# An adaLN Mamba and mixture-of-experts block: the small products of dt, router logits and sums of squares gathered into one row per pair of tiles

## Reference

```python
dt = jax.nn.softplus(dt + dt_bias)
y  = _ssd(x, dt, A, Bm, Cm) + x * D
y  = y * silu(z)
y  = y * rsqrt(mean(y * y, axis=-1) + EPS) * norm_w
x  = x + ga * (y @ W_out)
gate_logits = softmax(h2 @ gate_w + gate_b)
out = sum_e weights[:, e] * (h2 @ expert_w[e] + expert_b[e])
```

## Time and profile before

| what | value |
| --- | --- |
| runs | 2198.18, 2197.79, 2201.4 us, median 2198.18 |
| the profiled execution | span 2195.2 us from first to last instruction |
| what lies around the span, against the median | 3.0 us |
| PE busy | 2138.3 us (97%), 16090 matmuls |
| DVE, ACT, POOL busy | 1761.4 (80%), 1750.8 (80%), 1682.2 (77%) |
| mean granted TensorE clock | 0.992 of full |

### The profile page before, as it was taken

One profiled execution on the slowest core, in us unless ns is written; L12 is line 12 of the kernel. 1 busy time (PEld: TensorE's weight loads), 2 busy tenths in 40 slices (PEclk: granted clock), 3 DMA queues, 4 the chain that ended last, 5 costly groups with the idle time before them and its releaser, 6 DMA issues.

```text
span 2195.2 us, 51248 instructions
## 1 busy us (share of the span) xinstructions
PE 2138.3 (97%) x16090; PEld 1781.6 (81%) x16090; DVE 1761.4 (80%) x4001; ACT 1750.8 (80%) x4402; POOL 1682.2 (77%) x1812
## 2 busy tenths in 40 slices
PE   6799999999999999999999999999999999999997
PEld 5678888888888888888888888888888888888875
DVE  7778778887778888788888788888788887788863
ACT  5788887888887888888888888888888888888872
POOL 3568787777787777787777787777787777787786
PEclk9899999999999999999999999999999999999998
DMA  4221222222222222222222222222212222222210
GB/s 138 88 78 52 83 62 66 88 79 64 83 62 67 88 79 63 83 62 67 88 75 67 83 62 67 88 74 68 83 62 67 88 70 72 80 65 67 78 56 20
DMA packets 152204, 161.03 MB, mean 73 GB/s; under 512 B 15128, under 2 KB 134528, under 8 KB 151936
## 3 DMA queue, kind: packets, MB, share of 16 engines
q1 hardware_dynamic: 150160, 157.63, 23.4%
q10 hardware_dynamic: 1776, 0.12, 0.1%
HBM read 139.88 MB, written 17.83 MB: 72 GB/s over the span
## 4 chain that ended last, share of the span: by engine, by line
PE 89%; issue 3%; POOL 3%; DVE 3%; ACT 2%; DMA 0%; POOLq 0%; SPq 0%; DVEq 0%; ACTq 0%
PE pe L1320 32%; PE pa L1320 22%; PE pd L1320 12%; PE px L1320 10%; PE py L1320 6%; PE px L1432 3%; PE pa L1338 1%; PE pd L1491 1%; DVE feat L933 1%; PE py L1423 1%; POOL xd L423 0%; POOL ex L474 0%; POOL ex L479 0%; POOL ex L485 0%; POOL ex L470 0%
## 5 line engine op out<-in xcount | busy, mean ns | idle before, releaser
L933 DVE SCALAR_TENSOR_TENSOR feat<-pa,cw,feat 128x512 f32<-128x512 f32 x567 | 423.8, 747 | 83.5 <-ACT feat L609 73.1
L1320 PE MATMUL pe<-e_hi,h_hi 128*128 128x512 f32 x1024 | 443.7, 433 | 3.7 <-DVE eacc L1124 2.0
L1320 PE MATMUL pe<-e_lo,h_hi 128*128 128x512 f32 x1024 | 405.2, 396 | 0.0
L1320 PE MATMUL pe<-e_hi,h_lo 128*128 128x512 f32 x1024 | 404.4, 395 | 0.0
L1320 PE MATMUL pa<-h_hi,w_hi 128*128 128x260 f32 x1260 | 371.8, 295 | 6.3 <-DVE feat L933 5.7
L1320 PE MATMUL pa<-h_hi,w_lo 128*128 128x260 f32 x1260 | 357.8, 284 | 0.0
L1320 PE MATMUL pa<-h_lo,w_hi 128*128 128x260 f32 x1260 | 357.0, 283 | 0.0
L681 ACT ACTIVATE lm<-lm,lndt 128x128 f32<-128x128 f32 x1024 | 329.7, 405 | 2.5
L671 ACT ACTIVATE lm<-lm,e3in 128x128 f32<-128x128 f32 x1024 | 324.6, 405 | 1.1 <-DMA lm<-cs_rows 1.1
L761 ACT ACTIVATE ex<-pe,wg 128x256 f32<-128x256 f32 x512 | 215.0, 478 | 114.7 <-PE pe L1320 93.1
L1124 DVE SCALAR_TENSOR_TENSOR eacc<-pe,wg,eacc 128x256 f32<-128x256 f32 x512 | 244.3, 477 | 31.8 <-PE pe L1320 22.8
(11 more groups left out here) (184 smaller groups left out, 5659.3 us busy)
## 6 DMA issues: line engine op xcount, KB each, us to landing
lm<-cs_rows SPq DMA_DIRECT2D x128, 512.0 KB, 4.0
ebc<-cs_rows SPq DMA_DIRECT2D x256, 128.0 KB, 3.6
xin<-_attn_hidden_states_dram SPq DMA_DIRECT2D x32, 512.0 KB, 5.1
xres<-_attn_hidden_states_dram SPq DMA_DIRECT2D x128, 128.0 KB, 3.7
out_dram<-x SPq DMA_DIRECT2D x128, 128.0 KB, 3.9
gz<-in_L_wmod_dram SPq DMA_DIRECT2D x2, 512.0 KB, 8.2
ex<-in_L_ffn_expert_w_dram SPq DMA_DIRECT2D x1, 1024.0 KB, 11.5
x<-in_L_ffn_expert_w_dram SPq DMA_DIRECT2D x1, 1024.0 KB, 13.9
```

What stands on the lines that cost most here:

```text
L933: dve.scalar_tensor_tensor(out=acc, in0=proj_bank(x, i)[:, :, 1 + j:1 + j + HT], scalar=cw[:, f, j:j + 1], in1=acc, op0=ALU.mult, op1=ALU. ...
L1320: return pe.matmul(o, lhsT=l, rhs=r, start=start, stop=stop, skip_group_check=True)
```

## The change

Steps `dtm`, `dt2`, `lgm_`, `lg2`, `ssr_`, `ss_` on PE, `dte`, `lge`, `sre_` on ACT and `dtb`, `lg_`, `sse_` on DVE go. In their place stands one chain per pair: `mix`, `mixe`, `mix2`, `mixr`. `mix` of index c adds into the same four strips of `pd[:, 0]` the dt products of pair c+3, the logit products of pair c-1 and the sums of squares of pair c, each with 32-column weights that are zero outside their own rows. `mix2` turns them with 48 moving columns.

```diff
+            def mix(pe, c):
+                parts = [(slice((2 * a + k) * 32, (2 * a + k + 1) * 32), a, k) for a in range(2) for k in range(KT)]
+                sources = []
...
+                if c + 3 < NPAIR:
+                    pe.wait_ge(S["n_h"], c + 4)
+                    sources.append(lambda a, k: (wdt[:, k], hf[:, k, a * P:(a + 1) * P]))
...
+                if c >= 1:
+                    pe.wait_ge(S["h2e"], c)
+                    sources.append(lambda a, k: (wgate[:, k], h2f[:, k, a * P:(a + 1) * P]))
+                if 0 <= c < NPAIR:
+                    pe.wait_ge(S["sq"], 2 * (c + 1))
+                    sources.append(lambda a, k: (onec[:], y4[:, a, k * P:(k + 1) * P]))
+                    sources.append(lambda a, k: (onec[:], y4[:, a, (KT + k) * P:(KT + k + 1) * P]))
+                for i, source in enumerate(sources):
+                    for part, a, k in parts:
+                        last = mm_(pd[part, 0, 0:P], *source(a, k), i == 0, i == len(sources) - 1)
+                last.then_inc(S["mix"], 1)
...
+            def mix2(pe, c):
...
+                pe.wait_ge(S["mixe"], c + 4)
+                mm_(pd[:, 0, P:P + 2 * MIX], qs[:], sel[:].rearrange("p a r -> p (a r)"), True, True).then_inc(S["mix2"], 1)
...
+            def mixe(act, c):
+                act.wait_ge(S["mix"], c + 4)
...
+                act.activation(qs[:], pd[:, 0, 0:P], ACT.Copy).then_inc(S["mixe"], 1)
```

`sq_` now squares `y4` in place, after `yhi_` and `ylo_`, and `y1_` of the tile two later waits for `mix`. `rs_` runs once per pair. `x2_` waits for both output products of its pair; `wout_` has an output half for each tile. `cs_` takes a padded weight of 128 columns. `hT_` writes to `pd[:, 0]` and no longer to `pa`, shares it with `h2T_` and `mix`, and waits for `mixr`:

```diff
-                mm_(pa[cs_rows, 1, 0:P], flat, tri[:], True, True).then_inc(S["cs"], 1)
+                mm_(pa[:, 1, 0:P], dA_pad[:], tri[:], True, True).then_inc(S["cs"], 1)
...
             def sq_(act, x):
-                act.wait_ge(S["y4"], x.n + 1)
-                if x.n >= 1:
-                    act.wait_ge(S["ssr"], x.n)
-                act.activation(ysq[:], y4[:, x.j], ACT.Square, scale=DI ** -0.5).then_inc(S["sq"], 1)
+                act.wait_ge(S["y_hi"], x.n + 1)
+                act.wait_ge(S["y_lo"], x.n + 1)
+                act.activation(y4[:, x.j], y4[:, x.j], ACT.Square, scale=DI ** -0.5).then_inc(S["sq"], 1)
...
-                if x.t:
-                    pe.wait_ge(S["n_h"], x.pair)
-                elif x.g >= 1:
-                    pe.wait_ge(S["gzs"], 2 * x.g)
+                if x.pair >= 2:
+                    pe.wait_ge(S["mixr"], x.pair)
...
             def x2_(dve, x):
-                dve.wait_ge(S["wout"], x.n + 1)
-                dve.wait_ge(S["rs"], x.n + 1)
+                dve.wait_ge(S["wout"], 2 * (x.pair + 1))
+                dve.wait_ge(S["rs"], x.pair + 1)
```

All five lists are written anew. Most steps are labelled four tiles later (`ft` at n-8 and experts from n-16, where they stood at n-4 and n-12 before), with the distances between them nearly kept. PE's new list, in which `mix` stands twice and neither time beside `ydiag_`:

```diff
+                do(G_, pe, n - 10)
+                do_mix(mix, pe, n - 12)
+                do(xT_, pe, n - 10)
+                do_mix(mix2, pe, n - 12)
+                do(e0, pe, n - 16)
...
+                do(e3_, pe, n - 16)
+                do(cs_, pe, n - 8, T)
+                do(yoff_, pe, n - 9)
...
+                do(ydiag_, pe, n - 9)
+                do(hT_, pe, n - 4, T)
...
+                do(G_, pe, n - 8)
+                do(h2T_, pe, n - 12)
+                do(bias_, pe, n - 14)
+                do(wout_, pe, n - 9)
+                do(ft5, pe, n - 8, T)
+                do_mix(mix, pe, n - 10)
+                do(e0, pe, n - 14)
+                do_mix(mix2, pe, n - 10)
...
+                do(z_, pe, n - 6, T)
+                do(yoff_, pe, n - 7)
+                do(e1, pe, n - 13)
+                do(ft0, pe, n - 4, T)
+                do(e0, pe, n - 13)
+                do(ydiag_, pe, n - 7)
+                do(h2T_, pe, n - 10)
+                do(wout_, pe, n - 8)
+                do(e3_, pe, n - 13)
+                do(state_, pe, n - 7)
+                do(e2, pe, n - 13)
```

ACT's list, its parts around the changes of table (`use_table` loads one for SiLU before `si0`, `si2`, `gzs` and one for exp before `Lxa`, `Lxb`, `ln_*` when the other is in place):

```diff
+                do(si0, act, n - 8, T)
...
+                do(Lxa, act, n - 8)
...
+                do(si2, act, n - 8, T)
...
+                do(Lxa, act, n - 7)
...
+                do(gzs, act, n - 6, T)
+                do(sq_, act, n - 8)
+                do(xA0, act, n - 13)
+                do(La, act, n - 6)
+                do(ca0, act, n - 4, T)
+                do(Lxa, act, n - 6)
+                do(Lb, act, n - 6)
+                do(yhi_, act, n - 7)
+                do(h2, act, n - 10)
+                do(xA1, act, n - 13)
+                do(sq_, act, n - 7)
+                do(Lxb, act, n - 6)
```

More of the change, by code:

```diff
@@ L526, in _ @@
[L526 to L538, removed]
@@ new lines, in _ @@
+                do(bias_, act, n - 16)
+                do(ca2, act, n - 8, T)
+                do(xA0, act, n - 16)
+                do(ln_w, act, n - 8, T)
+                do(xt_, act, n - 9)
+                do(ln_dt, act, n - 8, T)
+                do(csT_rows, act, n - 8, T)
+                do(xA1, act, n - 16)
+                do(bt_, act, n - 9)
+                do(ca3, act, n - 8, T)
+                do(decays, act, n - 8, T)
+                do(yhi_, act, n - 10)
+                do(xA0, act, n - 15)
@@ new lines, in _ @@
+                do(si0, act, n - 8, T)
+                do(La, act, n - 8)
+                do(Lb, act, n - 8)
+                do(xA1, act, n - 15)
+                do(sq_, act, n - 10)
+                do(yhi_, act, n - 9)
+                do(ca4, act, n - 8, T)
+                do(n_h, act, n - 4, T)
+                do(si1, act, n - 8, T)
+                do(sq_, act, n - 9)
+                do(h2, act, n - 12)
+                do(Lxa, act, n - 8)
+                do(ca5, act, n - 8, T)
+                do(bias_, act, n - 14)
@@ new lines, in _ @@
+                do_mix(mixe, act, n - 10)
+                do(Lxb, act, n - 8)
+                do(bt_, act, n - 8)
+                do(si2, act, n - 8, T)
+                do(La, act, n - 7)
+                do(xA0, act, n - 14)
+                do(xt_, act, n - 8)
+                do(gzs, act, n - 8, T)
+                do(Lb, act, n - 7)
+                do(Lxa, act, n - 7)
+                do(n_h, act, n - 2, T)
+                do(Lxb, act, n - 7)
+                do(xA1, act, n - 14)
+                do(yhi_, act, n - 8)
@@ L882, in _ @@
-                do(Lb, act, n - 3)
-                do(lge, act, n - 8)
-                do(gzs, act, n - 2, T)
-                do(Lxa, act, n - 3)
-                do(n_h, act, n, T)
-                do(sq_, act, n - 4)
-                do(Lxb, act, n - 3)
-                do(dte, act, n, T)
-                do(xt_, act, n - 3)
-                do(xA0, act, n - 9)
-                do(n_h, act, n + 2, T)
-                do(h2, act, n - 6)
         @block.vector
@@ L1568, in _ @@
             do(hT_, pe, 0)
-            do(dtm, pe, 0)
             do(hT_, pe, 2)
-            do(dt2, pe, 0)
-            do(dtm, pe, 2)
-            do(dt2, pe, 2)
+            mix(pe, -3)
+            mix2(pe, -3)
+            mix(pe, -2)
+            mix2(pe, -2)
             do(ft0, pe, 0)
@@ L1647, in _ @@
-                do(yoff_, pe, n - 4)
-                do(z_, pe, n - 2, T)
-                do(lg2, pe, n - 8)
-                do(ydiag_, pe, n - 4)
-                do(hT_, pe, n, T)
-                do(state_, pe, n - 4)
-                do(e1, pe, n - 9)
-                do(G_, pe, n - 3)
-                do(e0, pe, n - 9)
-                do(xT_, pe, n - 3)
-                do(dtm, pe, n, T)
-                do(ssr_, pe, n - 4)
-                do(h2T_, pe, n - 6)
-                do(hT_, pe, n + 2, T)
```

652 lines of the change are left out of this document (284 added, 368 removed).

## The result

The changed kernel takes 2186.22 us (median of four runs, 2185.19 to 2188.7), the kernel before 2198.27 beside it: a ratio of 0.9945, with an interval of 0.9934 to 0.9957. It is faster, by 12 us where I had forecast 82, and outside the range. The profiled execution spans 2187.0 us, 8.2 less than that of before. It was the slowest of the four (2188.7), 2.5 us above the median, so its rows show a little less of the gain.

The account below looks back on a forecast made before the run. PE's instruction list was taken to bound the kernel. Savings of 1.32 + 0.52 + 0.20 + 0.22 + 0.31 = 2.57 us a group, 82 us over 32 groups, took 2198 to 2116 us, range 2096 to 2148.

Parts of the forecast that it names:

- I cost all this at nothing: ACT, DVE and POOL: their changed work, with two more ACT table loads a group, stays hidden behind PE; 0 us.
- I take 0: SP's `put_cs` behind two loads: sums reach the first `decay` in some 6.3 us, no wait; up to 1 us a group otherwise.
- The padded product, 0.31 us a group: Third product of the cumulative sums on PE: 128-column padded weight takes 0.22 instead of 0.53 us.
- 0 within 4 us: One-off memsets and the other order of the loop's head and tail: no cost, within 4 us.
- the rows of 1.01 us: PE's 32-column products: two runs of four rows at 1.01 us each, middle rows 0.22; saves 0.52 us a group.
- a table load without a drain: ACT: each table load costs its 1283 ns with no drain behind; 191 loads expected.
- no wait at `mix`: PE's `mix(n-12)` doesn't wait for `sq_`, with under 1 us of room.
- The six products fewer: PE's products with 128-column weights: six fewer a group at 0.22, saving 1.32 us.
- Rival 1: Other engines, mainly ACT with its table loads, give back 0.5 to 1.5 us a group: 2132 to 2164 us; chance 0.13.
- Rivals 2, 3 and 4: ACT idle after table loads (0.03, 2180 us); middle rows at 0.35 (0.05, 2133); `mix` waiting for the square (0.06, 2212).

Follow-up runs that it names:

- after: The changed kernel itself, as first measured against the kernel before: 2186.22 us, ratio 0.9945.
- pool_wait: The changed kernel with GpSimd held off until DVE's four small steps that make dA are done; 2198.45 us, ratio 0.9996 to the kernel before.
- pool_sp: pool_wait and sp_first together on the changed kernel; 2166.42 us, ratio 0.9851 to the kernel before.
- cs_late_sp: sp_first with the state's rows (`yoff_`) put ahead of the cumulative sums on PE; 2182.45 us, ratio 0.9924 to the kernel before.
- cs3_sp: cs_late_sp with expert product `e1` ahead of `ft3` on PE and ACT's evacuation of the last expert's bank moved earlier; 2209.6 us, ratio 1.005.
- cs3_swap: cs3_sp with DVE's `y_lo` ahead of the step that releases GpSimd's `h_lo`; 2187.07 us, ratio 0.9951 to the kernel before.
- sp_first: The changed kernel with SyncE's write and load of the decay rows ahead of the residual reload; 2183.08 us, ratio 0.9923 to the kernel before.
- before_pad: The kernel before with only the third product of the cumulative sums padded to 128 weight columns; 2201.74 us, ratio 1.0017.
- pool_unpad: pool_sp with the third product of the cumulative sums unpadded, 32 weight columns again; 2165.62 us, ratio 0.9845 to the kernel before.
- head: The changed kernel with an order of its own for the first scan pass on PE and ACT, tile 0's scan first; 2180.52 us, ratio 0.9922.
- pool_head: pool_sp with the first scan pass in the order of head; 2160.05 us, ratio 0.9823 to the kernel before, the fastest version.

## Why the prediction was wrong

The forecast had 82 us less: 74.5 in the 29 periods between tile 8 and tile 124, and the rest at the ends. The diagonal of tile 8 starts at 184.4 us before and 192.0 after, that of tile 124 at 2099.2 and 2083.0, and the spans end at 2195.2 and 2187.0. So the steady part gave 23.8 us and the ends took 15.6 back.

- **"I cost all this at nothing"** (the other engines), the step that failed most. It rested on shares of busy time, and these came out as said (after: DVE, ACT and POOL at 85%, 86% and 77% of 926 us). That was luck: they are shares of a period of 65.2 us. ACT's work is 56.3 us a group, not 55.3, and DVE's 55.7, more than the 54.2 of before, though it lost six small instructions; in the forecast period of 63.5 they would be 89% and 88%. And a share says nothing of a place. The sums start 0.94 us later behind the product ahead of them in each group, 27 us in all. I had looked at ACT, because of its tables; it was DVE, whose instructions I took at their old lengths. I counted its instructions and neither where its small steps would stand against PE's list, rewritten whole, nor what GpSimd would have in hand at the same moment. The 4.46 us of room that they had before were gone, and then the blocking counted. That the blocking makes them late is shown (pool_wait, pool_sp). That moving PE's steps alone does not win the time back is what cs_late_sp, cs3_sp and cs3_swap show; an order that would was not found.
- **"I take 0"** for the moved write of the decay rows. From the start of the sums to the landing of the first load pass 6.7 to 7.9 us in the groups of after without such trouble and 8.4 to 8.9 in the seven where the write lands late (forecast: "some 6.3", of parts that add to 6.0). It is not 0, but not the 10 us I later gave it either: sp_first gains 3 to 5. Its larger effect is on others: without it GpSimd's wait gains nothing, with it 20 us.
- **The padded product, 0.31 us a group** (10 us over 32 groups). Worth nothing in either order (before_pad, pool_unpad). The products themselves do get shorter, 0.66 us from the first to the state's rows in pool_sp for 0.79 in the earlier trace rows. But `ft3` behind waits for DVE's copy of the bank, as cs_late_sp shows it does when it comes early, so time saved there is likely waited away. In the old order the padding costs 3.5 us, 0.11 a group; in the changed one nothing. By the rule of the Trainium skill, TensorE: Matmul & The Clock Gate, LDWEIGHTS, that I had weighed and set aside, the estimate was a loss of 0.16: nearer to the runs than my 0.31 of gain; before_pad agrees with its sign.
- **"0 within 4 us"** for head and tail. It was 16. The loop runs every pass with one list, and in the first the later groups' work, and `mix2`, stood ahead of tile 0's scan. The run head gives back 6 us (tile 0 starts 4.0 us earlier, tile 8 3.2). The mean granted clock of the first 136 us was 0.91 before, 0.87 after and 0.86 in pool_head; what that costs in the head was not separated. The tail, where a pair's `x2` now waits for both tiles and their sum of squares, is 8 us longer, 4 of them idle time; it was only read, no run tried it.
- **Right:** the rows of 1.01 us (middle rows 0.22), a table load without a drain (189 loads of 1283 ns, I had said 191), no wait at `mix`. The six products fewer are in the count (376 fewer matmuls, 384 forecast); their price of 0.22 was not measured by itself. Rival 1, waits of 0.5 to 1.5 us a group, named the size and the wrong engine; its upper end, 2164, still counted neither the ends nor the padding. Rivals 2, 3 and 4 didn't happen.

The steady part missed 50.7 us. Its idle time grew by 31 us, and PE's busy time fell by 1.90 us a group and not by 2.57, which is the other 19. By cause, as read from the trace of after: 27 at the sums, some 10 in the long groups (7.6 in named waits, and what they delay, an estimate), 9 for the padding, and the 5 that are left over. These shares are bookkeeping: in pool_head, where the waits of the first two are gone, 21 of their 37 us came back. **What stays open:** pool_head has 3.1 us of named waits left and a period of 64.48 us (in an execution 5 us above its median), where the forecast without the padding would be 63.8. I read the 0.7 us as start-to-start delays below 0.3 us each, at `h2T_`, `state_` and `yoff_` among others; no run took them apart. Nor did one show why cs3_swap, without the old stall, is no faster than after.

## What to carry to other kernels

When the bounding engine's list gets shorter, price the others by place and not by share: for each product, which instruction of which engine releases it, and what has to run before that one. Before DVE and GpSimd are put side by side at 80% busy, see which of their instructions meet where something waits; a small instruction that hands over to PE should not stand beside a long one of GpSimd. Moves that pay nothing alone can pay together, so when a wait changes its name, take away the second one before giving the first up.

## What I had not expected of the hardware

- The blocking between DVE and GpSimd goes by who comes first, and a lead of 0.05 us is enough: `y_lo` lasts 0.69 us when it starts 0.05 us ahead of `h_lo` (after), and 1.69 when 0.15 behind (cs3_sp). A DVE instruction of 0.19 us lasted 1.00.
- A table load costs its 1283 ns and no more that the trace shows: behind every load of after the next activation starts within 0.05 us, mostly 0.01.
- Holding GpSimd idle for about 1 us in each group made the kernel 17 us faster (pool_sp against sp_first), although the instructions held back are as many as before.
